# Edge type masks from a DMA transpose, multiplied from SBUF, in a new order with a merged prologue

## The chip, the core and the metric

The kernel runs on one core of one Trainium2 chip. A core has five engines with a queue of their own each: TensorE (PE; its weight loads are listed apart as PEld), VectorE (DVE), ScalarE (ACT), GpSimd (POOL) and SyncE (SP), which here only issues DMAs. An engine works through its own queue in order and waits on semaphores for the others. SBUF is the on-chip memory, PSUM holds what PE writes. The metric is the device time of one launch in microseconds (us), lower is better. Three runs of the kernel before took 2405.45, 2407.12 and 2411.77 us; the median is 2407.12.

## The reference, cut to what matters

`x` holds 128 graphs of 128 nodes with 256 features, `adj` an integer 0 or 1 for each pair of nodes. Two layers follow each other. Layer 0 is an attention whose probabilities are split by edge type: for each type r the probabilities are masked with `adj == r` and meet a value projection of their own.

```
q, k   = heads(x @ Wq + bq), heads(x @ Wk + bk)          # 8 heads of 32
attn   = softmax(q k^T / sqrt(32))
out    = sum over r in 0..3 of (attn * (adj == r)) @ heads(x @ Wv[r] + bv[r])
x1     = layernorm(x + out @ Wo + bo) * g1 + beta1
x2     = layernorm(x1 + gelu(x1 @ W1 + b1) @ W2 + b2) * g2 + beta2
# layer 1
e      = leaky(q1 k1^T, 0.2) of x2, -9e15 where adj <= 0
h      = softmax(e) @ v1
y      = layernorm(concat(layernorm(h) * g1 + b1, x2) @ Wffn^T) * g2 + b2 + x2
```

## The kernel before, in words

The 128 graphs are worked through as 64 pairs (G = 2 graphs, 256 rows). Every engine has a function `steps(n)` written out by hand, called for n = 0 to 70. It lists the operations of one round with the pair that each is for (`n - 3` is the pair that entered three rounds ago), so that several pairs are under way at once, at different depths. The order inside `steps` is the order of the engine's queue. `PE_BANKS` says which of the eight PSUM banks each PE job uses, and from that table the PE queue derives which earlier result must have been read before a bank is written again.

To keep precision, every operand of a matrix product is held as a high half in fp16 and the rest, also in fp16. ACT makes the high half, and DVE or POOL subtract it from the source for the low half (`low`, L939 on DVE where the source lies in PSUM, L1178 on POOL where it lies in SBUF). SP then transposes the pair of halves by DMA into the layout that PE needs (L427 for rows, L470 and L477 for probabilities).

The edge types go this way. POOL compares the 128x256 integers of a pair with 0, 1, 2 and 3 (`edge_types`, L1186, four instructions). PE transposes the eight 128x128 masks into PSUM bank 2 (`transpose_edges`, L554). DVE multiplies them with the transposed probabilities (`by_edge_type`, L973, four instructions of 4096 elements per partition: two graphs, high and low half), and PE forms the products with the values (`attend_0`, L621). In L973 one factor, `pT`, is in SBUF, and the other, `edges`, in PSUM:

```
edges = ps("edges")[:].bitcast(F16).rearrange("p (g r j) -> p g r j", g=G, r=REL)
...
V_.tensor_tensor(pm0[g][:, s], pT0[g][:, s].unsqueeze(1).broadcast_to([P, REL, HEADS, P]),
                 edges[:, g].unsqueeze(2).broadcast_to([P, REL, HEADS, P]), ALU.mult)
```

Two DVE operations read and write nothing but SBUF tiles with one tensor input and a scalar: `no_edge` (L946, which makes layer 1's mask from the integers) and `attention_normed_1` (L1028). `max_1` (L952) reduces an SBUF tile to a maximum.

Before the pairs start, a block of its own loads all weights and biases, splits the weights into halves on ACT (L305) and DVE (L331), folds a gain into `Wffn` and transposes it on PE (L340, L345). All engines meet at its end; then the first pair's `x` is loaded (L414).

## Time and profile before

| | us |
|---|---|
| median of three runs | 2407.12 |
| the profiled execution, its own time | 2403.04 |
| span of its trace | 2401.2 |
| PE busy | 2284.4 (95%) |
| DVE busy | 2115.4 (88%) |
| ACT busy | 2120.3 (88%) |
| POOL busy | 1698.0 (71%) |

The span is the time from the first to the last instruction of the trace. The granted TensorE clock was 0.989 of full speed over the span. A busy share is an average over three stages: the prologue (to 34.8 us), the filling and draining of the pipeline, and the long steady part in which one round follows the other. The chain that ended last has 56% PE, 6% ACT and 6% DMA. In an answer of the trace, a group's "idle before" is the time that its engine stood idle just in front of its instructions.

### The profile page before, as it was taken

The page shows a single profiled execution, that of the slowest core. Times are in us where ns is not written, and L with a number is a line of the kernel's source. Part 1 is how long each engine was busy: PE and PEld are TensorE (multiplying, and loading weights), DVE is VectorE, ACT ScalarE, POOL GpSimd, SP SyncE. Part 2 cuts the span into 40 slices and gives each one's busy share as a digit, 9 for nine tenths or more (in the row PEclk, how much of TensorE's full clock was granted, in tenths as well). Part 3 has the DMA queues.
Part 4 walks back from the last instruction along what each step waited for, and adds up shares of the span by engine and source line. Part 5 has one row for each costly group of instructions (what it writes and reads, how often), then busy time and mean ns, then how long its engine had stood idle before and what let it go on. Part 6 is the DMA issues. An engine that isn't in the chain of part 4 may idle for free.

```text
span 2401.2 us, 80726 instructions
## 1 busy us (share of the span) xinstructions
PE 2284.4 (95%) x30284; PEld 1850.1 (77%) x30284; DVE 2115.4 (88%) x3987; ACT 2120.3 (88%) x5976; POOL 1698.0 (71%) x1870
## 2 busy tenths in 40 slices
PE   2799999999999999999999999999999999999984
PEld 1577888788788788788788887877877877877863
DVE  3779999999999999999999999999999998998973
ACT  4689999998999999999899999999999999999973
POOL 1467777777777777777777777777777777777763
PEclk9999999999999999999999999999999999999997
DMA  4447557657667666756756765766665675675553
GB/s 132 87 89 141 106 115 137 113 110 133 115 112 130 121 111 124 129 110 117 138 107 115 138 114 109 133 120 106 130 125 107 124 132 109 115 142 103 108 99 67
DMA packets 948549, 280.53 MB, mean 117 GB/s; under 512 B 877249, under 2 KB 947393, under 8 KB 948161
## 3 DMA queue, kind: packets, MB, share of 16 engines
q1 hardware_dynamic: 944992, 271.95, 61.0%
q8 instruction: 243, 3.98, 0.7%
q10 hardware_dynamic: 3168, 3.41, 0.5%
q14 instruction: 146, 1.19, 0.2%
HBM read 40.38 MB, written 16.78 MB: 24 GB/s over the span
## 4 chain that ended last, share of the span: by engine, by line
PE 56%; ACT 6%; DMA 6%; SPq 3%; issue 3%; DVE 2%; POOL 1%; DVEq 0%; ACTq 0%; POOLq 0%
PE bank L523 43%; PE bank L621 6%; PE bank L584 4%; DMA pT<-p1h 3%; ACT bank L778 3%; DMA xT<-x_rows 2%; PE bank L602 1%; SPq L477 1%; SPq L470 1%; ACT p0h L849 1%; ACT p L767 1%; SPq L427 1%; POOL x_rows L1178 1%; PE bank L554 1%; PE bank L569 1%
## 5 line engine op out<-in xcount | busy, mean ns | idle before, releaser
L973 DVE TENSOR_TENSOR pm<-pT,bank 128x4096 f16<-128x4096 f16 x256 | 573.4, 2277 | 9.8 <-DMA pT<-p0h 9.4
L523 PE MATMUL bank<-wv,xT 128*128 128x512 f16 (+1 forms) x2304 | 449.6, 345 | 0.0
L778 ACT ACTIVATE bank<-bank,p_nmax 128x128 f32<-128x128 f32 x1024 | 355.8, 369 | 23.9 <-DVE p_nmax L959 19.4
L1178 POOL TENSOR_TENSOR h<-h_f,h 128x512 f16<-128x512 f32 x256 | 292.6, 1164 | 96.6 <-ACT h L754 96.5
L523 PEld LDWEIGHTS bank<-wv,xT 128*128 128x128 f16 x2304 | 220.8, 98 | 178.3 <-issue 18.2
L523 PE MATMUL bank<-yT,w 128*128 128x256 f16 x3072 | 356.7, 273 | 0.3 <-DMA yT<-x_rows 0.2
L523 PE MATMUL bank<-w,h 128*128 128x256 f16 x3072 | 345.7, 272 | 2.7 <-POOL h L1178 2.7
L1178 POOL TENSOR_TENSOR x_rows<-x,x_rows 128x512 f16<-128x512 f32 x128 | 148.2, 1157 | 270.2 <-ACT x_rows L821 157.6
L767 ACT ACTIVATE p<-p,p_nmax 128x128 f32<-128x128 f32 x1024 | 336.5, 435 | 0.8
L523 PEld LDWEIGHTS bank<-yT,w 128*128 128x128 f16 x3072 | 295.3, 98 | 41.8 <-issue 0.8
L523 PEld LDWEIGHTS bank<-w,h 128*128 128x128 f16 x3072 | 295.9, 98 | 36.2 <-issue 2.8
L1178 POOL TENSOR_TENSOR p1h<-p,p1h 128x512 f16<-128x512 f32 x256 | 291.1, 1159 | 1.2 <-ACT p1h L808 1.2
L621 PE MATMUL bank<-v,pm 128*128 128x64 f16 (+1 forms) x8192 | 243.3, 183 | 0.6 <-issue 0.6
L778 ACT ACTIVATION_READ_ACCUMULATOR bank<-bank,p_nmax 128x1 f32 x1024 | 241.9, 236 | 0.0
L621 PEld LDWEIGHTS bank<-v,pm 128*128 128x128 f16 x8192 | 230.4, 96 | 8.4 <-issue 0.8
L523 PE MATMUL bank<-xT,wq 128*128 128x256 f16 x1536 | 191.2, 275 | 46.0 <-DMA xT<-x_rows 45.8
L1186 POOL TENSOR_SCALAR edge_rows<-adj_i 128x256 f16<-128x256 int32 x256 | 213.6, 852 | 22.0 <-PE bank L554 18.0
L959 DVE TENSOR_REDUCE p_nmax<-bank 128x4 f32<-128x512 f32 x256 | 169.0, 681 | 59.6 <-PE bank L584 59.5
L939 DVE TENSOR_TENSOR v<-bank,v 128x512 f16<-128x512 f32 (+1 forms) x384 | 212.0, 593 | 7.7 <-ACT v L814 2.7
L746 ACT ACTIVATE h_f<-bank,bff_col 128x256 f32<-128x256 f32 x512 | 213.4, 485 | 0.8
L523 PEld LDWEIGHTS bank<-xT,wq 128*128 128x128 f16 x1536 | 147.6, 98 | 67.6 <-issue 21.7
L523 PE MATMUL bank<-xT,wk 128*128 128x256 f16 x1536 | 193.2, 277 | 0.0
(125 smaller groups left out, 4888.6 us busy)
## 6 DMA issues: line engine op xcount, KB each, us to landing
x_sb<-in_x_dram SPq DMA_DIRECT2D x64, 256.0 KB, 3.0
adj_i<-in_adj_dram SPq DMA_DIRECT2D x128, 128.0 KB, 2.7
out_dram<-x2b SPq DMA_DIRECT2D x64, 256.0 KB, 3.0
xT<-x_rows SPq DMA_TRANSPOSE x128, 3.2
pT<-p0h SPq DMA_TRANSPOSE x128, 4.6
oT<-o_rows SPq DMA_TRANSPOSE x128, 3.2
pT<-p1h SPq DMA_TRANSPOSE x128, 5.0
pm<-in_L_gnn_W_dram ACTq DMA_DIRECT2D x1, 1024.0 KB, 13.1
```

Source lines behind the costliest of these rows:

```text
L427: sp.dma_start_transpose(to[:].rearrange("p s k (g t) -> p (s k g) t", g=G), rows[:].rearrange("p s k g c -> p (s k g c)")).then_inc(lande ...
L523: last = nc.tensor.matmul(o, l, r, start=(first and k == 0), stop=(final and k == len(todo) - 1))
L584: last = nc.tensor.matmul(ps(f"s{layer}_{r}")[:, at:at + P], q[rows, c, g * P:(g + 1) * P], k[rows, c, g * P:(g + 1) * P], start=first, st ...
L621: last = nc.tensor.matmul(to, pm0[g][:, s, r, hd], v, start=(r == 0 and s == 0), stop=(r == REL - 1 and s == 0))
L746: last = nc.scalar.activation(h_f[:, c], ps(f"h_{i}")[:, (c % 2) * T:(c % 2 + 1) * T], ACT.Gelu, bias=bff_col[:, c:c + 1])
L767: last = nc.scalar.activation(p1[:, r, g, c], p1[:, r, g, c], ACT.Exp, bias=p1_nmax[:, r, g, c:c + 1])
L778: last = nc.scalar.activation(ps(f"s0_{r}")[:, at:at + P], ps(f"s0_{r}")[:, at:at + P], ACT.Exp, bias=p0_nmax[:, r, g, c:c + 1], accum_out ...
L939: return V_.tensor_tensor(to, source, high, ALU.subtract)
L959: V_.tensor_reduce(flat(p0_nmax[:, r]), ps(f"s0_{r}")[:].rearrange("p (g j) -> p g j", j=P), AX_X, ALU.max, negate=True).then_inc(S["p0_ma ...
L973: V_.tensor_tensor(pm0[g][:, s], pT0[g][:, s].unsqueeze(1).broadcast_to([P, REL, HEADS, P]), edges[:, g].unsqueeze(2).broadcast_to([P, REL ...
L1178: return V_.tensor_tensor(to, source, high, ALU.subtract)
L1186: last = V_.tensor_scalar(edge_rows[:, :, r], adj0_i[:], float(r), None, ALU.is_equal)
```

## The change

Five things change together.

- **Masks.** POOL casts the integers of a pair to fp16 (`types_half`, 128x256), SP transposes the two 128x128 blocks by DMA (`transpose_types`), and POOL compares the transposed fp16 tile with 0 to 3 (`edge_types`, four instructions as before). The masks then lie in SBUF in the layout that DVE needs. `transpose_edges` on PE is gone, and so are the bank `edges` and its waits. `by_edge_type` reads both factors from SBUF.
- **Order.** All five `steps` are written in a new order, with other depths (DEPTH 6 instead of 7) and another bank table. On PE the feed-forward product and the first two value products of a round move to its end.
- **Prologue.** The block of its own is gone. The loads of `x`, `wq0`, `wk0` and the first integers come first in the queues; the halves of the first layer's attention weights are made on ACT and DVE at the head of their queues, and those of the later weights on ACT after the first pair's probabilities, and on POOL in `x_low(1)`. `Wffn` is folded on POOL and DVE in the first rounds and transposed by DMA.
- **Small tiles.** The layer norms' variances are turned into their inverse roots in place; some constants share a tile; scratch of the prologue lies in other tiles.
- **Waits.** For the first pair (m = 0) the queues wait for the pieces of the prologue that they need.

```
-        edges = ps("edges")[:].bitcast(F16).rearrange("p (g r j) -> p g r j", g=G, r=REL)
+        edges = edge_rows
...
                 def load_adj0(m):
                     if past(m):
+                        sp.wait_ge(S["adj0_half"], m)
+                        types_from_adj(m)
+
+                def transpose_types(m):
+                    sp.wait_ge(S["adj0_half"], m + 1)
+                    if past(m):
                         sp.wait_ge(S["adj0_masks"], m)
-                    sp.dma_start(adj0_i[:], adj_d[bass.ds(m * G, G)].rearrange("g t j -> t g j")).then_inc(S["adj0_in"], 16)
+                    sp.dma_start_transpose(adjT0[:], adj0_h[:].rearrange("p g j -> p (g j)")).then_inc(S["adjT0_in"], 16)
...
-                def transpose_edges(m):
-                    bank_free("edges", m)
-                    pe.wait_ge(S["adj0_masks"], m + 1)
-                    for g in range(G):
-                        for r in range(REL):
-                            last = nc.tensor.transpose(edges[:, g, r], edge_rows[:, g, r], ident_h[:])
-                    last.then_inc(S["edges_ps"], 1)
...
                 def by_edge_type(m, g, s):
 
                     dve.wait_ge(S[f"pT0_in_{g}"], 16 * m + 16)
-                    dve.wait_ge(S["edges_ps"], m + 1)
+                    dve.wait_ge(S["adj0_masks"], m + 1)
...
+                def later_weights_low():
+                    for n, (name, tile) in enumerate(later_parts):
+                        pool.wait_ge(s_hi1, n + 1)
+                        low(tile[:, 1], staged[name], tile[:, 0]).then_inc(s_lo1, 1)
+
+                def types_half(m):
+                    pool.wait_ge(S["adj0_in"], 16 * m + 16)
+                    if past(m):
+                        pool.wait_ge(S["adjT0_in"], 16 * m)
+                    V_.tensor_copy(adj0_h[:], adj0_i[:]).then_inc(S["adj0_half"], 1)
+                    if m == 0:
+                        fold_gain()
+
                 def edge_types(m):
-                    pool.wait_ge(S["adj0_in"], 16 * m + 16)
-                    if past(m):
-                        pool.wait_ge(S["edges_ps"], m)
+                    pool.wait_ge(S["adjT0_in"], 16 * m + 16)
+                    if past(m):
+                        pool.wait_ge(S["p0_masked"], 4 * m)
                     pool.sem_inc(s_apart)
                     for r in range(REL):
-                        last = V_.tensor_scalar(edge_rows[:, :, r], adj0_i[:], float(r), None, ALU.is_equal)
+                        last = V_.tensor_scalar(edge_rows[:, :, r], adjT0[:], float(r), None, ALU.is_equal)
                     last.then_inc(S["adj0_masks"], 1)
...
                 def x_low(m):
                     u = m % XR
                     pool.wait_ge(S["xT0_hi"], m + 1)
                     low(x_rows[:, 1], by_chunk(x_sb[u][:]), x_rows[:, 0]).then_inc(S["xT0_lo"], 1)
+                    if m == 1:
+                        later_weights_low()
...
+                rows_from_x(0)
+                load_weight(sp, "wk0")
+                types_from_adj(0)
...
+                sp.wait_ge(S["xT0_lo"], 1)
+                transpose_rows(xT0, x_rows, S["xT0_in"])
...
+                load_weight(sp, "wo0")
+                load_weight(sp, "wffn")
...
+                for name in ("w1", "w2", "wq1", "wk1", "wv1"):
+                    load_weight(sp, name)
...
+                def first_weights_high():
+                    for n, (name, tile) in enumerate(first_parts):
+                        act.wait_ge(landed_w[name], count_w[name])
+                        if n == 0:
+                            act.wait_ge(s_scaled, 3)
+                        nc.scalar.activation(tile[:, 0], staged[name], copy).then_inc(s_hi0, 1)
```

On DVE, in one round of the kernel before, the stretch around the four multiplications with the edge masks (`pm<-pT,bank`, L973; `v<-bank,v` are low halves of values, `x2b<-bank,w_rs,x2b` the output rows):

```order
L939 TENSOR_TENSOR v<-bank,v 128x16x32
L939 TENSOR_TENSOR v<-bank,v 128x8x32 x2
L973 TENSOR_TENSOR pm_0<-pT_0,bank 128x4096
L1046 SCALAR_TENSOR_TENSOR x2b<-bank,w_rs,x2b 128x256 x2
L973 TENSOR_TENSOR pm_0<-pT_0,bank 128x4096
L973 TENSOR_TENSOR pm_1<-pT_1,bank 128x4096 x2
L952 TENSOR_REDUCE p_nmax<-p 128x4
L946 TENSOR_SCALAR neg_mask<-adj_i 128x256
```

The same stretch of the DVE queue after the change (the multiplications are L971, `low` is L937):

```order
L937 TENSOR_TENSOR v<-bank,v 128x16x32
L971 TENSOR_TENSOR pm_0<-pT_0,edge_rows 128x4096 x2
L937 TENSOR_TENSOR v<-bank,v 128x8x32 x2
L1031 BN_AGGR ln_mean<-ln_stats 128x2 x2
L1048 SCALAR_TENSOR_TENSOR bank<-bank,ln_mean,g2b_row 128x256 x2
L971 TENSOR_TENSOR pm_1<-pT_1,edge_rows 128x4096 x2
L950 TENSOR_REDUCE p_nmax<-p 128x4
L1058 SCALAR_TENSOR_TENSOR x2b<-bank,ln_mean,x2b 128x256 x2
```

The second factor is now the SBUF tile `edge_rows`; the four multiplications stand in two pairs with layer 1's values and the last layer norm between them.

On POOL, in a round before, from the low halves of layer 1's probabilities (`p1h<-p,p1h`) through the comparisons (`edge_rows<-adj_i`) to those of the hidden layer (`h<-h_f,h`):

```order
L1178 TENSOR_TENSOR p1h<-p,p1h 128x2x2x128 x3
L1216 TENSOR_SCALAR w_ve<-w_mv 128x2
L1218 TENSOR_TENSOR w_rs<-w_ve,minus_half 128x2
L1228 TENSOR_TENSOR x1b<-x,b_row 128x512
L1186 TENSOR_SCALAR edge_rows<-adj_i 128x2x128 x4
L1209 TENSOR_TENSOR x_sb<-x_sb,bo_row 128x512
L1178 TENSOR_TENSOR h<-h_f,h 128x512 x4
```

And in a round after (`low` is L1206, the comparisons L1239, the cast L1229):

```order
L1239 TENSOR_SCALAR edge_rows<-adjT 128x2x128 x4
L1273 TENSOR_SCALAR ln_mean<-ln_mean 128x2
L1275 TENSOR_TENSOR ln_mean<-ln_mean,columns 128x2
L1206 TENSOR_TENSOR x_rows<-x_0,x_rows 128x512
L1206 TENSOR_TENSOR p1h<-p,p1h 128x2x2x128
L1206 TENSOR_TENSOR x_rows<-x,x_rows 128x512
L1285 TENSOR_TENSOR x1b<-x,b_row 128x512
L1206 TENSOR_TENSOR p1h<-p,p1h 128x2x2x128
L1229 CAST adj_h<-adj_i 128x256
L1206 TENSOR_TENSOR p1h<-p,p1h 128x2x2x128 x2
L1273 TENSOR_SCALAR ln_mean<-ln_mean 128x2
L1275 TENSOR_TENSOR ln_mean<-ln_mean,columns 128x2
```

The comparisons move to the end of POOL's round, a cast is added, and the low halves of the probabilities stand behind the second and third layer norm. The four `h<-h_f,h` follow right behind the last row.

## Rows read from the trace of the kernel before

**Rows 1.** Chain of waits, 1005 to 1046 us: start us, us, what.
```profile
1004.87 0.86 PE bank L523 x4
...
1009.88 0.45 PE bank L554 x8
...
1045.08 0.45 PE bank L554 x8
```

**Rows 2.** Busy time by windows: stretch, its us, then each engine, clock, DMA share.
```profile
1005.70:1040.90 35.20, 35.20 (x475) 28.71 (x473) 32.73 (x63) 32.81 (x95) 26.47 (x30) 1.00 0.63 122
sum 105.60, PE 105.60 PEld 86.06 DVE 98.15 ACT 98.32 POOL 79.23; mean PE 35.20 PEld 28.69 DVE 32.72 ACT 32.77 POOL 26.41
...
1013.50:1023.20 9.70, 9.70 (x123) 8.17 (x122) 9.70 (x8) 8.04 (x17) 8.68 (x11) 1.00 1.12 205
```

**Rows 3.** Timeline of PE, L678: its first and its 59th of 64.
```profile
186.90 0.38 PE L678 MATMUL bank<-w_bias,ones 128*128 128x512 f16 x1
...
2250.87 0.38 PE L678 MATMUL bank<-w_bias,ones 128*128 128x512 f16 x1
```

**Rows 4.** Four DVE lines: count, ns min/median/max, first and last start.
```profile
L973 DVE TENSOR_TENSOR pm<-pT,bank x256: 2272/2277/2289, 64.3 to 2301.4; 128x4096 f16<-128x4096 f16 x128
...
L946 DVE TENSOR_SCALAR neg_mask<-adj_i x64: 278/535/1253, 102.3 to 2332.1; 128x256 bf16<-128x256 int32 x64
...
L1028 DVE TENSOR_SCALAR o<-o,o_mv,o_rs x128: 398/410/839, 177.2 to 2384.2; 128x256 f32<-128x256 f32 x128
...
L952 DVE TENSOR_REDUCE p_nmax<-p x256: 665/675/687, 134.1 to 2366.1; 128x4 f32<-128x512 f32 x128
```

**Rows 5.** Timelines of DVE and POOL around two L946.
```profile
631.93 1.25 DVE L946 TENSOR_SCALAR neg_mask<-adj_i 128x256 bf16<-128x256 int32 x1
...
951.32 0.28 DVE L946 TENSOR_SCALAR neg_mask<-adj_i 128x256 bf16<-128x256 int32 x1
...
630.75 2.28 POOL L1178 TENSOR_TENSOR h<-h_f,h 128x512 f16<-128x512 f32 x2 [1.61 <-ACT h L754]
...
950.18 2.43 POOL L1178 TENSOR_TENSOR h<-h_f,h 128x512 f16<-128x512 f32 x2 [1.73 <-ACT h L754]
```

**Rows 6.** Groups by line and shape: busy us, mean ns, idle before, releaser.
```profile
L331 DVE TENSOR_TENSOR w<-pm,w 128x2048 f16<-128x2048 f32 x2 | 4.5, 2284 | 0.0
...
L1186 POOL TENSOR_SCALAR edge_rows<-adj_i 128x256 f16<-128x256 int32 x256 | 213.6, 852 | 22.0 <-PE bank L554 18.0
...
L269 POOL CAST ident_h<-ident 128x128 f16<-128x128 f32 x1 | 0.3, 293 | 0.0
...
L1178 POOL TENSOR_TENSOR x_rows<-x,x_rows 128x512 f16<-128x512 f32 x128 | 148.2, 1157 | 270.2 <-ACT x_rows L821 157.6 <-ACT x_rows L842 112.6
...
L1209 POOL TENSOR_TENSOR x_sb<-x_sb,bo_row 128x512 f32<-128x512 f32 x64 | 81.5, 1273 | 0.0
...
L1198 POOL TENSOR_TENSOR o<-o,p_rsum 128x512 f32<-128x512 f32 x64 | 67.1, 1048 | 134.8 <-DVE o L998 134.8
```

**Rows 7.** Timeline of the prologue and the first pair, several engines.
```profile
25.88 3.69 ACT L305 ACTIVATE w<-pm 128x2048 f16<-128x2048 f32 x2
...
34.79 0.39 SPq L414 DMA_DIRECT2D x_sb<-in_x_dram  x1
...
48.43 1.17 PE L584 MATMUL bank<-k,q 32*128 32x128 f32 x32 [1.02 <-ACT k L787]
...
57.57 1.29 DVE L939 TENSOR_TENSOR p0h<-bank,p0h 128x512 f16<-128x512 f32 x2 [1.88 <-ACT p0h L849]
...
64.32 4.47 DVE L973 TENSOR_TENSOR pm<-pT,bank 128x4096 f16<-128x4096 f16 x2
```

**Rows 8.** DMA issues: KB each, us to landing.
```profile
adj_i<-in_adj_dram SPq DMA_DIRECT2D x128, 128.0 KB, 2.7
...
xT<-x_rows SPq DMA_TRANSPOSE x128, 3.2
...
pm<-in_L_gnn_W_dram ACTq DMA_DIRECT2D x1, 1024.0 KB, 13.1
```

More of the change, by code:

```diff
@@ L140, in build @@
         edge_rows = sb("edge_rows", [G, REL, P], F16)
+        adj0_h, adjT0 = (sb(n, [G, P], F16) for n in ("adj0_h", "adjT0"))
         adj1_i = sb("adj1_i", [G, P], I32)
@@ L164, in build @@
         h = sb("h", [2, FC, T], F16)
-        x2 = [sb(f"x2_{u}", [G, D]) for u in range(2)]
+        x2 = [sb(f"x2_{u}", [G, D]) for u in range(X2R)]
         v1 = sb("v1", [2, G, HEADS, DH + 1], F16)
@@ L211, in build @@
[L211 to L217 removed]
+        at = place("wq0", stage0, 0, KC, D)
@@ new lines, in build @@
+        at = place("wk0", stage0, at, KC, D)
+        at = place("wo0", stage0, at, KC, D)
+        at = place("wv0", stage0, at, KC, V)
+        at = place("w1", p1_flat, 0, KC, FF)
+        at = place("w2", pT1_flat, 0, FC, D)
+        at = place("wq1", p1h_flat, 0, KC, D)
+        at = place("wk1", p1h_flat, at, KC, D)
+        at = place("wv1", p1h_flat, at, KC, D)
+        at = place("wffn", hf_flat, 0, KC, 2 * D)
+        at = place("shifted", hf_flat, at, KC, D)
+        g1_row1, b1_row1 = hf_flat[:, at:at + D], hf_flat[:, at + D:at + 2 * D]
@@ new lines, in _ @@
+                load_weight(sp, "wo0")
+                load_weight(sp, "wffn")
+                sp.dma_start(b1_row1, row(a["L1_gnn_b1"])).then_inc(s_ends, 16)
+                sp.dma_start(g1_row1, row(a["L1_gnn_g1"])).then_inc(s_ends, 16)
+                rows_from_x(1)
+                for name in ("w1", "w2", "wq1", "wk1", "wv1"):
+                    load_weight(sp, name)
+                for tile, v in late_rows:
+                    sp.dma_start(tile[:], row(a[v])).then_inc(s_rows, 16)
@@ L539, in transpose_rows @@
                             at = (c * G + g) * P
-                            last = nc.tensor.transpose(o[:, at:at + P], src[:, g, c * P:(c + 1) * P], ident[:])
+                            last = nc.tensor.transpose(o[:, at:at + P], src[:, g, c * P:(c + 1) * P], ident)
                     return last
@@ L986, in values_low_1, with fold_shift @@
                     last.then_inc(S["v1_lo"], 1)
+                def fold_shift():
+                    dve.wait_ge(s_fold, 1)
+                    V_.tensor_reduce(shift_cols, staged["shifted"], AX_X, ALU.add).then_inc(s_shift, 1)
+                    dve.wait_ge(s_shift, 1)
+                    high, rest = (shift_rows.rearrange("p (o j) -> p o j", o=KC)[:, :, at] for at in (0, DH))
+                    dve.wait_ge(s_const, CONSTANTS)
+                    V_.tensor_copy(high, shift_cols).then_inc(s_shift, 1)
+                    dve.wait_ge(s_shift, 2)
+                    low(rest, shift_cols, high).then_inc(s_shift, 1)
                 def recip_0(m):
@@ L1045, in scaled_added @@
                     for g in range(G):
[L1046 removed]
+                        last = V_.scalar_tensor_tensor(to[:, g], rows_in(name, g), mv[:, g, 1:2], added(g), ALU.mult, ALU.add)
                     return last
@@ new lines, in steps @@
+                    if live(n - 3):
+                        max_1(n - 3, 2)
+                    if live(n - 1):
+                        rows_x1(n - 1)
+                    if live(n):
+                        values_low_0(n, 0)
+                        values_low_0(n, 1)
+                        recip_0(n)
+                        values_low_0(n, 2)
+                    if live(n - 3):
+                        max_1(n - 3, 3)
+                    if live(n - 4):
+                        statistics("w", n - 4)
@@ new lines, in _ @@
+                dve.wait_ge(s_keyed, 32)
+                V_.tensor_scalar(bq_col, bq_col, SCALE, None, ALU.mult).then_inc(s_scaled, 1)
+                dve.wait_ge(landed_w["wq0"], count_w["wq0"])
+                V_.tensor_scalar(staged["wq0"], staged["wq0"], SCALE, None, ALU.mult).then_inc(s_scaled, 1)
+                dve.wait_ge(s_bv_hi, 1)
+                low(bv_lo, bv_f, bv_hi).then_inc(s_bv_lo, 1)
+                dve.wait_ge(s_scaled, 3)
+                for n, (name, tile) in enumerate(first_parts):
+                    dve.wait_ge(s_hi0, n + 1)
+                    low(tile[:, 1], staged[name], tile[:, 0]).then_inc(s_lo0, 1)
```

738 lines of the change are left out of this document (367 added, 371 removed).

## The prediction

> **What bounds the kernel now.** I read the chain of waits first, in a stretch of the steady part. It is PE from end to end: between the two edge transposes at 1009.88 and 1045.08 lies one round of 35.20 us, and no other engine stands in the chain; the eight transposes take 0.45 us of it [rows 1]. The busy times by windows say the same: over three such rounds PE is busy for 35.20 of 35.20 us, DVE 32.72, ACT 32.77, POOL 26.41 [rows 2]. So DVE has 2.48 us a round to spare, ACT 2.43, POOL 8.79. The rounds are not all that short: from the first to the 59th of the products that open the last projection, 58 rounds take 2063.97 us, 35.59 each [rows 3]; the 0.39 over 35.20 is what PE waits or runs longer in some rounds.
>
> **Masks, PE's part.** Eight transposes a round go. PE's own sum falls from 35.20 to 34.75. If PE stays the bound, that is 58 x 0.45 = 26 us. For that, DVE with 32.72 and ACT with 32.77 must still fit in, each with 2 us left; today they do with 2.4.
>
> **Masks, DVE's part.** The multiplication L973 has 4096 elements and takes 2272 to 2289 ns, in every one of 256 instances [rows 4]; L331, whose tensors are fp32, takes 2284 for half as many [rows 6]. So L973 runs at the double rate already with one factor in PSUM, and I expect no shorter instruction from SBUF. The Trainium skill (VectorE: DVE Perf Modes, section "The perf-mode tier table") has a rule that speaks the other way: a two-tensor operation with any operand in PSUM does one element a cycle, and two if all are 16-bit in SBUF. By it L973 would take 4.55 us now, at L331's rate, and the change would free some 9 us of DVE a round. The trace differs, 2.28 us, and the measurement decides.
>
> What changes is where L973 reads. Four DVE lines tell how that matters [rows 4]. L973 with one tile in SBUF and one in PSUM, and L952, which draws one SBUF tile at one element a cycle (512 in 675 ns), never wait. L946 and L1028, which have one SBUF tile but are faster per element (L946: 256 in 278 ns at best), spread from 278 to 1253 and from 398 to 839. The timelines show why [rows 5]: the L946 that started at 631.93 sat under a pair of POOL's subtractions and took 1.25 us; the one at 951.32 got in between and took 0.28, and POOL's pair needed 2.43 us instead of 2.28. In these forms DVE and POOL exclude each other, and whoever comes second waits; of the 0.28, POOL lost 0.15, so 0.13 is hidden in its own start.
>
> No row has a DVE instruction with two SBUF tensors beside a working POOL (L331 ran while POOL stood idle). The ends are: the new multiplication behaves as L952, and costs nothing; or as L946, and each of the four bars POOL for its 2.28 us and waits for POOL's current instruction, 0 to 0.97 us (1253 less 280). I take the second end, because the new form draws two SBUF streams at the double rate, nearer to the fast L946 than to the single stream of L952. On this the Trainium skill (SBUF — State Buffer, section "Who interferes with whom") is plain: a DVE instruction with two SBUF inputs contends with a GpSimd instruction that reads SBUF, and the loser is blocked for the whole instruction. By that page the second end holds; L946's spread agrees for its form, and no run here shows the two-input one.
>
> POOL's sum then is 26.41 for its work, some 0.45 for the new cast (128 elements take 0.29 [rows 6], so 0.29 to 0.59 for 256; I take the middle), and 4 x (2.28 - 0.13) = 8.6 of barred time: 35.5 us a round. The comparisons stay four, at 0.85 each as now [rows 6]; whether fp16 input is cheaper no row shows, so 0 to 1 us a round less. The barred time would cost nothing where POOL waits for data anyway, 8.79 us a round, most of it before the low halves of rows (270.2 us over 64 pairs, 4.2 each) and before L1198 (134.8, 2.1 each) [rows 6]. But those waits lie elsewhere: in the 9.70 us in which today's four multiplications run, POOL is busy for 8.68 [rows 2]. The new order does not empty that place: POOL has the low halves of the probabilities, the cast and the four of the hidden layer to do while DVE multiplies, as the two orders show. So POOL stays at 35.5 plus the part of its waits that is left over. I take 1.1 of the 8.79: 36.6 us. DVE's sum agrees: 32.72, plus four waits of about half of 0.97, is 34.7, and with 1.9 of its 2.48 us of waits it comes to 36.6 as well. The ends are 34.75 (PE alone) and 38.0 (POOL keeps 2.5 of its waits).
>
> A round of 36.6 against 35.59 is +1.0, in 58 rounds +58 us. PE's 0.45 is not subtracted again: PE would then wait.
>
> **Masks, the DMA.** One more transpose, of two blocks of 128x128, stands in SP's queue; one of eight blocks lands after 3.2 us [rows 8]. Load (2.7), cast (0.45), transpose (at most 3.2) and comparisons (4 x 0.85) are some 10 us in a row, and have most of a round, since POOL compares at the round's end for the next one. Behind it in SP's queue stand the transposes of layer 1's attention rows and of the next probabilities, which wait with it if the cast is late; DVE's multiplications wait for those. Costed at nothing; if that cover is gone, it is in the upper end.
>
> **Prologue.** Now the first x is requested at 34.79 us, the first scores are formed at 48.43 and the first multiplication starts at 64.32 [rows 7]. After, x is requested at the start, at about 0.7, and its probabilities need the same steps: their last low halves end 24.1 us after the request (57.57 + 1.29 - 34.79), and I add 6 us, since ACT must first see and cast three more weights. That makes 31. But POOL now has the low halves of the later weights in front of the first comparisons: ACT casts for 5.5 us (3.69 for the two large ones [rows 7], three of a quarter the size, some 0.6 each), then POOL subtracts two of 2048 elements and three of 512 at 1.16 us for 512 [rows 6], 12.7 us, from about 33 on; then 1.3 for the bias [rows 6] and 3.4 for the comparisons. The first multiplication can start at about 50, 14 us before today's. So 14 and not 34 us are gained. The ends: 28 if the head start of the scores (48.43 to about 20) carries through, 5 if the large weights, which take 13.1 us to land now [rows 8], hold ACT up for longer.
>
> **Order, depth, banks, small tiles.** I cost them at nothing: the sums of every engine are the same, and products that move on PE stand where its queue was full before. The cover for late inputs is the 2 us that DVE and ACT have; if it is gone, PE waits as in the 0.39 of today.
>
> **Sum.** Against the execution's own time of 2403 us: 2403 - 14 + 58 = 2447. The median of the runs is 4 us above that execution (2407.1), so the forecast is 2451. Its own range, for rounds of 36.0 to 37.4 (+24 to +105), is 2417 to 2498.
>
> **Rivals.**
> First, no exclusion: the new multiplications behave as L952. PE stays the bound, a round is 34.75 + 0.39 = 35.14: 2403 - 14 - 26 + 4 = 2367. L973's and L952's constant durations speak for it, L946's spread against. With the prologue's 28 it is 2353, and with all of the 0.39 gone 2330. It decides as soon as a round is under 35.83 (14 us over 58 rounds are 0.24): then the kernel is not slower.
> Second, exclusion that fits into POOL's waits: POOL comes to 35.5 with nothing left over, 2403 - 14 - 5 + 4 = 2388. For it speaks POOL's 8.79 us; against, the 8.68 of 9.70.
> Third, exclusion with a second wait behind it: two multiplications bar POOL while three low halves of layer 1's probabilities are due, these are 4.3 us late, then their transposes, and PE waits for them in `attend_1`. Rounds of 38.0: 2403 - 14 + 140 + 4 = 2533.
> That the change doesn't do what it says is not likely: the transposes on PE are gone by the order; only a late `adjT0` could hold the masks, and that is in the third.
>
> **Chances.** Forecast 0.48, first rival 0.25, second 0.12, third 0.15. About 0.3%, 7 us, is what a measurement of this kernel can tell from no change. Faster are the first two rivals, all but 0.03 of them, and 0.04 of the forecast's low tail: 0.38. Within 0.3%: 0.07, from the same borders. Slower: 0.55. The range runs from 2338, which leaves the first rival's best ends out, to 2522, just short of the third's full price.
>
> **What would show it.** By steps: no transposes of `edge_rows` on PE; the multiplication's durations spread from 2.27 to over 3 us, and POOL's subtractions beside it up to 3.3 us, where all are constant today; PE with gaps in the steady rounds, in front of the masked products; rounds of 36.6 us between the openings of the last projection; the first multiplication at about 50 us. The prediction is wrong if the multiplications keep 2.28 us with a narrow spread, or if POOL's are stretched and the rounds still come at 35.2 or less.

## The result, and the profile after

Four runs of the changed kernel took 2501.46 to 2508.51 us, median 2504.91; four of the kernel before on the same chip 2405.45 to 2411.77, median 2409.03. The ratio is 1.0391, interval 1.0367 to 1.0415: slower by 96 us, where the prediction said 44. The direction and the range (2338 to 2522) held; the size is off by more than half, and the forecast's own range (2417 to 2498) was missed by 7 us. The profiled execution took 2506.78 us, 103.7 more than that of before, which lay 6 us under its median; its span is 2505.0 us (2401.2 before).

First the stages. These are the first and the 59th opening of the last projection (L646) in the timeline of PE, the counterparts of [rows 3], and one line of the timeline of DVE, the first multiplications:

```profile
187.84 0.38 PE L646 MATMUL bank<-w_bias,ones 128*128 128x512 f16 x1
...
2343.71 0.38 PE L646 MATMUL bank<-w_bias,ones 128*128 128x512 f16 x1
...
51.19 9.00 DVE L971 TENSOR_TENSOR pm<-pT,edge_rows 128x4096 f16<-128x4096 f16 x4 [5.71 <-POOL edge_rows L1239]
```

58 rounds take 2155.87 us, 37.17 each against 35.59: +91.9. What lies ahead of the first opening is longer by 0.9 although the multiplication starts 13 us earlier (51.19 against 64.32), and what lies behind the 59th takes 161.3 us against 150.3. These three, +91.9, +0.9 and +11.0, are the 103.8 between the spans. The granted TensorE clock is 1.00 of full speed (2.4 GHz) in the 58 rounds of both kernels, so the clock doesn't explain the +91.9. It is lower after the change while the pipeline fills (0.85 on average against 0.94) and drains (0.87 against 0.89); what that adds to the +0.9 and the +11.0 was not separated.

Busy time by windows over three steady rounds (columns as in [rows 2]):

```profile
1011.00:1048.10 37.10, 35.75 (x468) 28.24 (x466) 35.10 (x63) 33.12 (x94) 34.82 (x31) 1.00 0.62 118
...
sum 111.30, PE 106.92 PEld 84.37 DVE 105.13 ACT 99.30 POOL 104.32; mean PE 35.64 PEld 28.12 DVE 35.04 ACT 33.10 POOL 34.77
```

POOL went from 26.41 to 34.77 us a round, DVE from 32.72 to 35.04. Both have 2 us left of 37.10, and PE is no longer busy throughout. The groups by line and shape show which operations grew (busy us, mean ns, idle before):

```profile
L971 DVE TENSOR_TENSOR pm<-pT,edge_rows 128x4096 f16<-128x4096 f16 x256 | 666.5, 2642 | 6.0 <-POOL edge_rows L1239 5.7 <-DMA pT<-p0h 0.2
L1206 POOL TENSOR_TENSOR p1h<-p,p1h 128x512 f16<-128x512 f32 x256 | 422.6, 1660 | 1.3 <-ACT p1h L796 1.2
...
L1275 POOL TENSOR_TENSOR ln_mean<-ln_mean,columns 128x2 f32<-128x2 f32 x256 | 294.6, 1151 | 21.3
L1239 POOL TENSOR_SCALAR edge_rows<-adjT 128x256 f16<-128x256 f16 x256 | 214.0, 853 | 7.2 <-DMA adjT<-adj_h 3.2
L1273 POOL TENSOR_SCALAR ln_mean<-ln_mean 128x2 f32<-128x2 f32 x256 | 177.0, 692 | 119.7 <-DVE ln_mean L1031 114.4
...
L1229 POOL CAST adj_h<-adj_i 128x256 f16<-128x256 int32 x64 | 153.4, 2397 | 0.0
```

A cast that takes 0.40 us in the prologue takes 2.40 here. The timelines of DVE and POOL over the same stretch show why (start, us):

```profile
1013.62 5.58 DVE L971 TENSOR_TENSOR pm<-pT,edge_rows 128x4096 f16<-128x4096 f16 x2
1020.85 4.85 DVE L971 TENSOR_TENSOR pm<-pT,edge_rows 128x4096 f16<-128x4096 f16 x2
...
1035.06 2.65 DVE L1038 TENSOR_SCALAR o<-o,ln_mean 128x256 f32<-128x256 f32 x2 [0.57 <-POOL ln_mean L1275]
...
1014.61 2.45 POOL L1229 CAST adj_h<-adj_i 128x256 f16<-128x256 int32 x1
1017.03 4.32 POOL L1206 TENSOR_TENSOR p1h<-p,p1h 128x512 f16<-128x512 f32 x2
1021.32 2.26 POOL L1273 TENSOR_SCALAR ln_mean<-ln_mean 128x2 f32<-128x2 f32 x1
1023.66 2.61 POOL L1275 TENSOR_TENSOR ln_mean<-ln_mean,columns 128x2 f32<-128x2 f32 x1
...
1034.99 1.29 POOL L1310 TENSOR_TENSOR x2b<-x,b2b_row 128x512 f32<-128x512 f32 x1
1036.22 1.33 POOL L1266 TENSOR_TENSOR x_sb<-x_sb,bo_row 128x512 f32<-128x512 f32 x1
1038.45 1.16 POOL L1206 TENSOR_TENSOR o_rows<-o,o_rows 128x512 f16<-128x512 f32 x1 [0.90 <-ACT o_rows L846]
1040.51 0.22 POOL L1273 TENSOR_SCALAR ln_mean<-ln_mean 128x2 f32<-128x2 f32 x1 [0.91 <-DVE ln_mean L1031]
```

Beside every multiplication one POOL operation stands still for about 2.0 us, whatever its size: the cast, one of the two `p1h`, L1273 and L1275. Even the two-element L1273 takes 2.26 where it takes 0.22 elsewhere. The line L971, with its spread (min/median/max), answers to [rows 4]; two other lines are there too:

```profile
L971 DVE TENSOR_TENSOR pm<-pT,edge_rows x256: 2276/2481/3249, 51.2 to 2397.4; 128x4096 f16<-128x4096 f16 x128
...
L1038 DVE TENSOR_SCALAR o<-o,ln_mean x128: 400/1355/1379, 177.2 to 2488.7; 128x256 f32<-128x256 f32 x128
...
L944 DVE TENSOR_SCALAR neg_mask<-adj_i x64: 284/555/1278, 95.8 to 2433.4; 128x256 bf16<-128x256 int32 x64
```

The minimum of the multiplication, 2276 ns, is that of before: its own speed has not changed. What I had not looked for is L1038, from a median of 410 to 1355: in the new order POOL's two additions (x2b, x_sb) stand right behind the inverse root that releases it.

PE's two largest waits over the rounds (total us, times, longest):

```profile
PE bank L524 <- DVE p0h L937: 30.9, 56, 0.9
PE bank L481 <- DMA pT<-p1h: 26.0, 31, 2.3
```

The first is not there in the kernel before: `p0h` follows L1038 in DVE's queue. The second, 7.7 us before, is the path of the third rival: `attend_1` waits for layer 1's probabilities. In the 58 rounds PE doesn't wait in front of the masked products, where the prediction looked for the gaps.

### The profile page after: what moved, and what is told of

Same layout as the page of the kernel before. It is cut to its first block and busy times, and to the rows that moved or that the text cites. A ratio compares the mean times of both kernels' runs of the same rounds, so it can differ in the third digit from the quotient of the medians.

```text
span 2505.0 us, 79871 instructions
## 1 busy us (share of the span) xinstructions
PE 2312.9 (92%) x29760; PEld 1822.1 (73%) x29760; DVE 2257.1 (90%) x3979; ACT 2132.7 (85%) x5963; POOL 2226.5 (89%) x1943
## 5 line engine op out<-in xcount | busy, mean ns | idle before, releaser
L971 DVE TENSOR_TENSOR pm<-pT,edge_rows 128x4096 f16<-128x4096 f16 x256 | 666.5, 2642 | 6.0 <-POOL edge_rows L1239 5.7
L1206 POOL TENSOR_TENSOR p1h<-p,p1h 128x512 f16<-128x512 f32 x256 | 422.6, 1660 | 1.3 <-ACT p1h L796 1.2
L755 ACT ACTIVATE p<-p,p_nmax 128x128 f32<-128x128 f32 x1024 | 325.8, 392 | 0.8
L1206 POOL TENSOR_TENSOR h<-h_f,h 128x512 f16<-128x512 f32 (+1 forms) x257 | 299.3, 1192 | 22.5 <-ACT h L740 22.1
L1275 POOL TENSOR_TENSOR ln_mean<-ln_mean,columns 128x2 f32<-128x2 f32 x256 | 294.6, 1151 | 21.3
L1273 POOL TENSOR_SCALAR ln_mean<-ln_mean 128x2 f32<-128x2 f32 x256 | 177.0, 692 | 119.7 <-DVE ln_mean L1031 114.4
L937 DVE TENSOR_TENSOR v<-bank,v 128x512 f16<-128x512 f32 (+1 forms) x384 | 212.9, 582 | 18.2 <-ACT v L822 13.3
L1239 POOL TENSOR_SCALAR edge_rows<-adjT 128x256 f16<-128x256 f16 x256 | 214.0, 853 | 7.2 <-DMA adjT<-adj_h 3.2
L730 ACT ACTIVATE h_f<-bank,columns 128x256 f32<-128x256 f32 x512 | 210.2, 482 | 1.1 <-PE bank L481 0.2
L1206 POOL TENSOR_TENSOR o_rows<-o,o_rows 128x512 f16<-128x512 f32 x128 | 147.8, 1155 | 60.3 <-ACT o_rows L846 58.5
L1038 DVE TENSOR_SCALAR o<-o,ln_mean 128x256 f32<-128x256 f32 x128 | 165.0, 1329 | 35.2 <-POOL ln_mean L1275 33.5
```

The lines of the kernel that those rows point to most:

```text
L730: last = nc.scalar.activation(h_f[:, c], ps(f"h_{i}")[:, (c % 2) * T:(c % 2 + 1) * T], ACT.Gelu, bias=bff_col[:, c:c + 1])
L755: last = nc.scalar.activation(p1[:, r, g, c], p1[:, r, g, c], ACT.Exp, bias=p1_nmax[:, r, g, c:c + 1])
L937: return V_.tensor_tensor(to, source, high, ALU.subtract)
L1038: V_.tensor_scalar(o1[:, g], o1[:, g], mv[:, g, 0:1], mv[:, g, 1:2], ALU.subtract, ALU.mult).then_inc(S["o1_normed"], 1)
L1206: return V_.tensor_tensor(to, source, high, ALU.subtract)
L1239: last = V_.tensor_scalar(edge_rows[:, :, r], adjT0[:], float(r), None, ALU.is_equal)
```

## Experiments

Each ran beside the kernel before on the same chip, whose median there was 2405.81 to 2410.23. "Round" is the mean of 58 between the first and the 59th opening of the last projection.

| run | us | ratio, interval | round |
|---|---|---|---|
| kernel before | 2409.03 | 1 | 35.59 |
| changed kernel | 2504.91 | 1.0391, 1.0367 to 1.0415 | 37.17 |
| 1 old order, factor from SBUF | 2715.44 | 1.1285, 1.1265 to 1.1304 | 40.54 |
| 2 new order, one input | 2425.75 | 1.0084, 1.0070 to 1.0097 | 35.90 |
| 3 new order, half of them two inputs | 2434.20 | 1.0119, 1.0106 to 1.0132 | 36.05 |
| 4 old order, merged prologue | 2396.09 | 0.9960, 0.9945 to 0.9974 | 35.62 |
| 5 changed, POOL line moved | 2551.55 | 1.0598, 1.0569 to 1.0628 | 38.04 |
| 6 as 2, POOL line moved | 2477.03 | 1.0278, 1.0263 to 1.0294 | 36.75 |
| 7 as 2, additions earlier | 3001.74 | 1.2458, 1.2439 to 1.2476 | 45.36 |
| 8 changed, additions earlier | 3028.85 | 1.2569, 1.2545 to 1.2593 | 45.84 |
| 9 as 2, additions apart | 2416.01 | 1.0035, 1.0020 to 1.0050 | 35.69 |
| 10 changed, one addition short | 2461.73 | 1.0224, 1.0197 to 1.0252 | 36.48 |
| 11 as 4, masks packed to the bank | 2393.18 | 0.9938, 0.9923 to 0.9953 | 35.48 |

**Is it the second SBUF input?** Run 1 changes one operand in the kernel before.

```
-                                     edges[:, g].unsqueeze(2).broadcast_to([P, REL, HEADS, P]),
+                                     ones16[:].unsqueeze(1).unsqueeze(1).broadcast_to([P, REL, HEADS, P]),
```

> The kernel before with one edit: DVE's four multiplications a round take their second factor from a constant SBUF tile of ones instead of the PSUM masks (so no probability is masked; PE still makes the masks). Order, prologue and counts are those of before. Exclusion between DVE and POOL: the multiplications spread from 2.28 to over 3 us, POOL's work beside them is stretched, rounds of 36.5 to 37.5 us instead of 35.6, time 2460 to 2530. New order as the cause: nothing changes here, multiplications all at 2.28, rounds 35.6, 2400 to 2415.

The mechanism holds, its price does not: 4.95 us a round, 310 us in all. The source view of the multiplication, and busy time by windows over about one round (columns as in [rows 2]):

```profile
L973 DVE TENSOR_TENSOR pm<-pT,ones x256: 2281/2478/3358, 64.0 to 2610.2; 128x4096 f16<-128x4096 f16 x128
```

```profile
1000.00:1040.80 40.80, 37.09 (x473) 29.67 (x473) 33.91 (x62) 33.12 (x94) 33.51 (x30) 0.96 0.58 105
```

Its neighbours on POOL, from the timeline:

```profile
1023.19 2.27 POOL L1216 TENSOR_SCALAR w_ve<-w_mv 128x2 f32<-128x2 f32 x1
...
1027.45 8.54 POOL L1186 TENSOR_SCALAR edge_rows<-adj_i 128x256 f16<-128x256 int32 x4
```

And PE's waits over the 58 rounds (total us, times, longest):

```profile
PE bank L523 <- POOL h L1178: 132.4, 58, 2.4
PE bank L584 <- DVE o L1089: 66.3, 56, 1.7
```

POOL is busy only 79% of the span, so it isn't full. But what it does beside the multiplications (the comparisons, 8.54 us instead of 3.40) stands ahead of the hidden layer's low halves, and PE waits for those in every round. Not all of the 4.95 us is such waiting. PE now stands idle for 3.7 of 40.8 us, its granted clock is 0.96 on average against 1.00 before, and it is busy for 37.09 us a round against 35.20. So up to 1.9 us of the price is PE itself being busy for longer at the lower clock.

Run 2 does the opposite in the changed kernel: a one-input operation of the same duration, on half as many elements, in place of the multiplication. The masking is left out.

```
-                    V_.tensor_tensor(pm0[g][:, s], pT0[g][:, s].unsqueeze(1).broadcast_to([P, REL, HEADS, P]),
...
+                    V_.tensor_reduce(pm0[g][:, s, 0:2], pT0[g][:, s].unsqueeze(1).broadcast_to([P, 2, HEADS, P]).unsqueeze(4),
+                                     AX_X, ALU.max).then_inc(S["p0_masked"], 1)
```

> The changed kernel with each multiplication replaced by a reduction over an axis of length one, from the SBUF probabilities alone (2048 elements, about the same 2.2 to 2.3 us; half of the masked tile is written, unmasked, the rest stays zero). All waits and the order stay, only the second SBUF stream goes. Exclusion: the operation no longer waits (spread under 0.05 us), POOL's cast is back at 0.4 us, rounds of 35.0 to 35.4, time 2365 to 2390; the 13 us of the earlier first multiplication stay visible at the first last projection (about 175 us instead of 188). New order as the cause: rounds stay near 37.1 and the time near 2500.

The page's busy times, the source view of the new operation, and POOL's cast beside two of them in the timeline:

```profile
PE 2288.7 (94%) x29760; PEld 1816.9 (75%) x29760; DVE 2208.8 (91%) x3983; ACT 2122.1 (88%) x5963; POOL 1745.4 (72%) x1943
```

```profile
L973 DVE TENSOR_REDUCE pm<-pT x256: 2227/2275/2286, 51.3 to 2315.4; 128x2048 f16<-128x2048 f16 x128
```

```profile
1014.66 0.41 POOL L1230 CAST adj_h<-adj_i 128x256 f16<-128x256 int32 x1
```

The spread is gone, the cast is back at 0.41, POOL's busy time falls from 2226.5 to 1745.4, and 79 of the 96 us go with them. By this run the exclusion costs 1.27 us a round in this order. But the time missed the expectation by 36 us to the slow side: without exclusion the new order is still not faster than the old one.

Run 3 keeps the two-input form for the high halves alone.

```
...
+                    if s == 1:
+                        V_.tensor_reduce(pm0[g][:, s, 0:2], pT0[g][:, s].unsqueeze(1).broadcast_to([P, 2, HEADS, P]).unsqueeze(4),
+                                         AX_X, ALU.max).then_inc(S["p0_masked"], 1)
+                        return
                     V_.tensor_tensor(pm0[g][:, s], pT0[g][:, s].unsqueeze(1).broadcast_to([P, REL, HEADS, P]),
```

> As the run with one stream, but only the two multiplications a round for the low halves are replaced; the two for the high halves still read two SBUF tiles. A lock that adds to POOL's round in proportion: POOL loses about 4 us a round instead of 8, rounds between 35.3 and 36.2, time 2385 to 2440. If one single wait at the end of the four decides instead of the sum, rounds stay at 37.1 or fall all the way to 35.2.

Half of the exclusion costs 8 us, the other half 71. POOL's busy share is 72% of the span with none of it, 79% with half and 89% with all. That fits a first half that goes into waits that POOL had, and a second that finds none left; no run tests it further.

**Is POOL's row the bound of the changed kernel?** Run 10 shortens one POOL operation that lies beside no multiplication; most of that addition is left out.

```
+                    some = slice(0, D if m == 0 else 16)
-                    V_.tensor_tensor(x1b[:], x1[:], both(b2_row), ALU.add).then_inc(S["x1_plus_b2"], 1)
+                    V_.tensor_tensor(x1b[:, :, some], x1[:, :, some], both(b2_row)[:, :, some], ALU.add).then_inc(S["x1_plus_b2"], 1)
```

> The changed kernel with one operation of GpSimd that lies beside no multiplication cut short: residual_bias_ff adds x1 and b2 on all 512 columns of a partition in the first block alone and on 32 in the others (left out: most of that residual), 1.26 us shorter by about 1.0 us. Nothing else changes, the lock of the multiplications included. Theory A (GpSimd's row bounds the round): the round is shorter by 0.8 to 1.2 us, 36.0 to 36.4 us, 2430 to 2460 us. Theory B (something else ends the round, GpSimd's length only coming out near it): rounds 36.9 to 37.2 us, 2490 to 2510 us.

From POOL's timeline, and the sum and mean of three rounds by windows:

```profile
1028.58 0.25 POOL L1286 TENSOR_TENSOR x1b<-x,b_row 128x32 f32<-128x32 f32 x1
...
1029.89 0.41 POOL L1229 CAST adj_h<-adj_i 128x256 f16<-128x256 int32 x1
...
1037.82 2.73 POOL L1206 TENSOR_TENSOR h<-h_f,h 128x512 f16<-128x512 f32 x1 [0.17 <-ACT h L740]
1041.44 4.53 POOL L1206 TENSOR_TENSOR h<-h_f,h 128x512 f16<-128x512 f32 x3 [0.89 <-ACT h L740]
```

```profile
sum 109.50, PE 106.67 PEld 84.59 DVE 108.13 ACT 99.01 POOL 97.70; mean PE 35.56 PEld 28.20 DVE 36.04 ACT 33.00 POOL 32.57
```

The operation fell from 1.26 to 0.25 us and the round from 37.17 to 36.48: 0.69 of the 1.01 us came back, somewhat less than expected, the time 2 us outside. So the round does hang on POOL's queue in the changed kernel. But the shorter operation also shifted what meets what: the cast is back at 0.41 us, POOL is busy for 32.57 us a round, 2.20 less than in the changed kernel, and it waits for ACT before the hidden layer's low halves (0.17 and 0.89 us here). DVE, its stretched multiplications included, is now busy for 36.04 of 36.50 us, against 35.04 of 37.10. So what takes over at 36.5 is probably DVE's queue and no longer POOL's; no run tested that.

Run 5 moves POOL's second low half of layer 1's attention up, in front of the two additions, so that L1038 stands free; run 6 does the same to the kernel of run 2.

```
                         rstd("o1", n - 5)
+                        attention_low_1(n - 5)
                         residual_shift_1(n - 5)
                     if live(n - 1):
                         residual_bias_0(n - 1)
-                    if live(n - 5):
-                        attention_low_1(n - 5)
```

> The changed kernel with one line moved: GpSimd issues attention_low_1(n-5) directly behind the rstd of the first output norm, ahead of residual_shift_1 and residual_bias_0, so that the additions of x (x2b, x_sb) no longer lie beside VectorE's pair of normed (L1038, 2 x 1.355 us there against 0.40 in the kernel before). Theory A (the round is set by GpSimd, 34.8 of 37.1 us busy, because its operations stand still beside the two-input multiplication): moving work within GpSimd's row takes away none of it, the rounds stay at 37.1 +- 0.3 us and the time at 2490 to 2515 us. Theory B (the round is set by the ring through normed, which loses 2 x 0.95 us under x2b and x_sb): the ring is shorter by up to 1.9 us, rounds 35.6 to 36.5, 2405 to 2465 us.

> The kernel of the second run (new order, the multiplication replaced by a one-input operation of about the same length; the masking is left out) with the same line of GpSimd moved. There GpSimd has slack (1745 us busy) and the rounds were 35.90 us against 35.59 in the kernel before. Theory A (what the new order costs without the lock is the ring through normed, held under x2b and x_sb): the ring goes, rounds 35.0 to 35.5 us, 2365 to 2405 us. Theory B (the order's price lies elsewhere, in the chain from o_lo over o_rows to the first scores, whatever normed takes): rounds stay at 35.8 to 36.1, 2420 to 2435 us.

Both theories missed in both runs. L1038 did go back to 0.41 us, but POOL now stands idle where the additions had been. From POOL's timeline in run 5:

```profile
1045.52 0.71 POOL L1275 TENSOR_TENSOR ln_mean<-ln_mean,columns 128x2 f32<-128x2 f32 x1
1049.09 1.16 POOL L1206 TENSOR_TENSOR o_rows<-o,o_rows 128x512 f16<-128x512 f32 x1 [2.86 <-ACT o_rows L846]
1050.20 1.30 POOL L1310 TENSOR_TENSOR x2b<-x,b2b_row 128x512 f32<-128x512 f32 x1
```

A wait of 2.86 us at the head of the queue, in place of 0.90, puts everything behind it late, the additions first. Rounds grew by 0.87 and 0.85.

Runs 7 and 8 moved the additions to POOL's waits ahead of the hidden layer instead, in the kernel of run 2 and in the changed one.

```
-                        residual_shift_1(n - 5)
-                    if live(n - 1):
-                        residual_bias_0(n - 1)
...
+                    if live(n - 5):
+                        residual_shift_1(n - 5)
                     if live(n - 3):
                         hidden_low(n - 3, 0)
+                    if live(n - 1):
+                        residual_bias_0(n - 1)
```

> The kernel of the second run (new order, one-input operation in place of the multiplication; the masking is left out) with GpSimd's two additions residual_shift_1 (x2b) and residual_bias_0 (x_sb) moved from behind the rstd of the first output norm to the two waits of 1.8 us that GpSimd has before hidden_low(0) and hidden_low(1). VectorE's pair of normed then has no GpSimd operation beside it, and attention_low_1 still comes before rstd f, but with nothing new in front of it. Theory A (what the new order costs without the lock is the ring of rstd, normed, first scores, held 2 x 0.95 us under x2b and x_sb): normed is back at 0.40 us, rounds 34.9 to 35.5 us against 35.90, 2360 to 2405 us. Theory B (the price is elsewhere in the ring, or GpSimd's hidden_low comes later by what is put in front of it): rounds 35.8 to 36.8 us, 2420 to 2480 us, as the fifth and sixth runs came out slower for what they delayed.

> The same two additions moved in the changed kernel itself, with its two-input multiplication. There GpSimd has no wait before hidden_low. Theory A (GpSimd's row bounds the round: 34.8 us busy and 1.8 us of waits): the two additions take their 2.6 us all the same, and GpSimd now stands 2.9 us before attention_low_1 (as in the fifth run) that the additions filled: rounds 38 to 39.3 us, 2545 to 2620 us. Theory B (the ring through normed bounds it): normed short, rounds 35.3 to 36.5 us, 2390 to 2465 us.

Both failed as tests by a dependency that I had overlooked: x2b's buffer is the one that the preceding pair's output is stored from, and that store hangs on the inverse root directly ahead. In run 7:

```profile
1014.37 0.72 POOL L1276 TENSOR_TENSOR ln_mean<-ln_mean,columns 128x2 f32<-128x2 f32 x1
1025.85 1.28 POOL L1311 TENSOR_TENSOR x2b<-x,b2b_row 128x512 f32<-128x512 f32 x1 [10.76 <-DMA out_dram<-x2b]
```

**What does the new order cost without the exclusion?** Run 9 avoids that dependency in the kernel of run 2: x_sb goes between the first two low halves of the hidden layer, x2b behind `attention_low_1`.

```
                         hidden_low(n - 3, 0)
+                    if live(n - 1):
+                        residual_bias_0(n - 1)
...
                         rstd("o1", n - 5)
+                        attention_low_1(n - 5)
                         residual_shift_1(n - 5)
-                    if live(n - 1):
-                        residual_bias_0(n - 1)
-                    if live(n - 5):
-                        attention_low_1(n - 5)
```

> The kernel of the second run (new order, one-input operation in place of the multiplication; the masking is left out) once more with GpSimd's two additions taken from beside normed, this time to places where the trace shows nothing late: x_sb into the 1.8 us wait ahead of the second hidden_low, x2b behind attention_low_1, into the 0.9 us wait ahead of rstd f, some 15 us behind the rstd w that its buffer's store hangs on (in the seventh run it stood right behind that rstd and waited 10.76 us for the store). Theory A (the new order's price without the lock is the ring rstd, normed, first scores, held under the two additions): normed back at 0.40 us, rounds 34.9 to 35.5 us against 35.90, 2365 to 2405 us. Theory B (the ring is held elsewhere): rounds 35.7 to 36.2 us, 2415 to 2445 us.

L1039 (L1038 of the changed kernel) and PE's waits over the rounds, of run 2 and then of run 9:

```profile
L1039 DVE TENSOR_SCALAR o<-o,ln_mean x128: 399/1352/1390, 173.5 to 2406.8; 128x256 f32<-128x256 f32 x128
```

```profile
PE bank L524 <- DVE p0h L937: 15.7, 58, 0.3
PE bank L481 <- DMA xT<-x_rows: 14.4, 18, 1.2
```

```profile
L1039 DVE TENSOR_SCALAR o<-o,ln_mean x128: 404/410/414, 179.9 to 2397.8; 128x256 f32<-128x256 f32 x128
```

```profile
PE bank L481 <- DMA xT<-x_rows: 9.5, 13, 1.4
PE bank L481 <- DMA yT<-x_rows: 5.7, 13, 0.9
```

The wait for p0h behind L1039 is gone, and with it 0.21 of the 0.31 us a round by which the new order was longer. The round, 35.69, fell between the two expectations; the time, 2416, is that of the second, since the first opening of the last projection comes at 189.0 instead of 182.9. The remaining 0.10 us is not explained by these runs.

**Prologue alone.** Run 4 is the kernel before with the merged prologue and the small tiles of the change; order, banks, depth and mask matmuls are the old ones (the prologue part of the change above; its head on SP):

```
+                rows_from_x(0)
+                load_weight(sp, "wk0")
+                types_from_adj(0)
```

> The merged prologue of the changed kernel with the order, the banks, the depth and the PSUM masks of the kernel before. If the head start of 13 us at the first multiplication is only lost to DVE and POOL excluding each other during the filling, it shows here: 2390 to 2398. If the filling itself absorbs any head start (the low halves of the later weights on POOL, PE's slower clock early on), 2403 to 2412.

```profile
176.88 0.38 PE L643 MATMUL bank<-w_bias,ones 128*128 128x512 f16 x1
...
2243.03 0.38 PE L643 MATMUL bank<-w_bias,ones 128*128 128x512 f16 x1
```

The first opening comes 10.0 us before that of [rows 3] and the rounds stay (35.62 against 35.59). The median, 2396, lies in the first expectation: 10 us under the kernel before. The profiled execution keeps 5 of them, since its rounds take 2 us more in all and the part behind the 59th opening 2.5. In run 2, with the new order and no exclusion, the first opening comes at 182.9, so the new order takes back some 6 of the 10 us while the pipeline fills. The changed kernel opens at 187.8; but run 5, with all of the exclusion and one POOL line moved, opens at 181.7, so the last 5 us can't be put down to the exclusion as such.

**What the masks on PE were worth.** Run 11 makes the masks as the change does, in the kernel of run 4, and has ScalarE copy them into the freed PSUM bank, so that the multiplication keeps one PSUM input; nothing is left out. The mask's fp16 pairs travel as int32 words.

```
+                    nc.scalar.activation(ps("edges")[:].bitcast(I32), edge_rows[:].rearrange("p g r j -> p (g r j)").bitcast(I32),
+                                         copy).then_inc(S["edges_ps"], 1)
```

> The kernel of the fourth run (the order of before, merged prologue) with the masks made as the change makes them (cast to fp16, transposed by DMA, compared by GpSimd), but multiplied from PSUM: ScalarE copies the compared masks, 1024 fp16 numbers of a partition taken as 512 int32 words, into the PSUM bank that the mask matmuls filled. Nothing is left out. The 8 mask matmuls of a block (0.219 us each in the trace of the fourth run, 1.75 us together) go, the multiplication keeps one input in PSUM. ScalarE gets one copy of 512 words a block (about 0.6 us by its 128x512 copies) where it waited 0.54 us. Theory A (TensorE's row bounds the old order's round, 35.2 of 35.6 us): rounds shorter by 0.7 to 1.75 us, 33.9 to 34.9 us, 2295 to 2355 us. Theory B (the ring of the old order stands at about the same length, the matmuls removed lay beside waits): rounds 35.3 to 35.9 us, 2375 to 2410 us. By either, GpSimd's operations beside the multiplication stay at their short times, unlike in the first run.

The source view of the multiplication, two openings of the last projection, and the mean of three rounds by windows:

```profile
L981 DVE TENSOR_TENSOR pm<-pT,bank x256: 2270/2278/2289, 51.4 to 2283.4; 128x4096 f16<-128x4096 f16 x128
```

```profile
174.47 0.38 PE L647 MATMUL bank<-w_bias,ones 128*128 128x512 f16 x1
...
2232.75 0.38 PE L647 MATMUL bank<-w_bias,ones 128*128 128x512 f16 x1
```

```profile
sum 106.50, PE 105.11 PEld 84.86 DVE 98.81 ACT 100.36 POOL 80.86; mean PE 35.04 PEld 28.29 DVE 32.94 ACT 33.45 POOL 26.95
```

No spread, POOL at 26.95 us a round, and rounds of 35.48: the second expectation. Taking the eight transposes off PE, with the copy (0.6 to 0.77 us) put on ACT, is worth 0.14 us a round here (35.62 to 35.48), not 0.45. The 1.75 us of the first expectation adds up durations that overlap on PE: in the chain the eight take 0.45 [rows 1]. How much the copy gave back was not separated. This version, 2393.18 us, is faster than both kernels, by 0.6% (0.5 to 0.8) than the one before; whether also than run 4, whose interval overlaps, is open.

## Why the prediction was right in kind and wrong in size

- **The exclusion: right.** The multiplication's spread (2276 to 3249 ns) and POOL's operations standing still beside it are there; run 1 switches them on with one operand and run 2 off. Not there are PE's gaps in front of the masked products: PE waits elsewhere. The rule of the Trainium skill (SBUF — State Buffer, section "Who interferes with whom") agrees with these rows. The other rule weighed, that a PSUM operand halves the multiplication's rate (VectorE: DVE Perf Modes, section "The perf-mode tier table"), does not: 2277 ns from PSUM and at best 2276 from SBUF. One reading on the way was wrong: L1028 is not faster per element than L952 (256 in 398 ns are 1.55 ns each, 512 in 675 are 1.32), and yet it spreads. So speed was not the mark to choose by; the choice came out right all the same.
- **The rounds: the term that was mis-sized.** "I take 1.1 of the 8.79: 36.6 us" is the step that failed, with the sum "+58 us" on it. POOL is busy for 34.8 us, 0.7 less than the 35.5 of the sum. But of its waits 2.3 us stayed, not 1.1; the smaller sum hid a part of that. So the round is 37.1: +91.9 instead of +58. Two waits of 0.9 us make up most of what stayed. One is before `o_rows`, for an ACT half that needs DVE's L1038; the other is before L1273, for DVE's L1031, which stands behind L1038 in DVE's queue with no idle time between them. L1038 itself starts from POOL's own inverse root and is drawn out beside POOL's additions. So a longer POOL row moves these waits along and doesn't fill them; that last step is read from the trace and not tested alone.
- **The third rival: partly there.** Its path, PE waiting in `attend_1` for `p1h`, took 26.0 us over the 58 rounds, 18 more than before, where the rival had 140.
- **Order at nothing: wrong.** "The sums of every engine are the same" was no reason. Without the exclusion the rounds are 0.31 us longer than before (18 us), though the masks are off PE; runs 4 and 11 clear the prologue, the small tiles and the new masks of that, so what is left is the order with its depth and banks. 0.21 of the 0.31 went when run 9 took two additions from beside L1038. The spread of that operation (L1028 before) stood in [rows 4]; the prediction used it to argue for the multiplication, and didn't ask where the new order puts L1038 itself.
- **Prologue: right where it was looked at, wrong as a term.** The multiplication starts at 51.19 (about 50 forecast), but "-14" was carried to the end of the sum. Of 13 us ahead at the first multiplication 10 are left at the first last projection in the old order, and none in the changed kernel. A head start counts only where the steady rounds begin.
- **End: missing.** The sum had no term for the drain, 161.3 us against 150.3. Run 2 has 158.3 without the exclusion. But run 11 has 158.4 in the old order, with the masks off PE, where run 4 has 152.9 with them on it. So the order isn't shown to be the cause, and which part of the change makes the 11 us stays open; each of these numbers is from one execution, and the six executions of run 4 differ by up to 9 us.
- **PE's part: not shown at its size.** The first rival and the low end of the range rested on rounds shorter by 0.45; run 11 shows 0.14, with a copy on ACT that the change doesn't have.

Against the forecast's +44, the rounds are 34 us longer, the drain adds 11 and the prologue's gain is missing with 15. These make 60 us, the whole difference from the +103.8 of the two spans.

## What to carry to other kernels

Before an operand is moved from PSUM to SBUF, look at what GpSimd does beside the VectorE instruction that reads it. If the form becomes one that excludes GpSimd, each instance bars it for nearly its whole length (here 1.99 of 2.28 us). The cost is what of that doesn't fall into GpSimd's waits, and what hangs on the operations that stand behind it. Four instances a round cost 1.3 us in one order and 5.0 in another (up to 1.9 of these by a slower PE), so the price goes by the place, not by the sum. And before a wait is counted as slack, look at who releases it: the two that stayed here hang on an operation that the stretched engine itself starts.

## What the runs showed of the hardware

- For the fp16 multiplication the exclusion comes with the second SBUF tensor, not with its rate: 4096 elements in 2277 ns with one factor in PSUM leave GpSimd alone (its comparisons take 0.85 us each), in 2276 ns at best from two SBUF tiles they bar it (a cast takes 2.40 us instead of 0.40). A one-input maximum of 2048 elements in 2275 ns leaves it alone too (the cast takes 0.41).
- A second tensor is not the only way in: L1038, one fp32 tensor of 256 elements and two scalars of its partition, takes a median of 1.35 us beside GpSimd's additions (run 2) and 0.41 where these are moved away (run 9).
- The two-input multiplication bars short work as long as large: a two-element operation took 2.26 us instead of 0.22, while a 512-element subtraction of 1.16 us took 3.2 at most; and POOL's busy time grew by 7.96 us a round beside the cast's own 0.40 (34.77 less 26.41 and 0.40), 1.99 for each multiplication of at least 2.28, so some of the bar is hidden, as in [rows 5].
- ScalarE copied 512 int32 words of packed fp16 pairs (masks of 0 and 1) into PSUM unchanged, in 0.6 to 0.77 us; VectorE then multiplied them as fp16 at the same 2.28 us.
